# Softmax row sums of an attention kernel: from fifteen additions on GpSimd to block sums on VectorE, with more split tiles and one buffer less

## What is computed

```
kv = concatenate([context, latents], axis=1)              # 1857 keys
q = rms_norm((latents @ Wq) split into 32 heads, q_norm_w)
k = rms_norm((kv @ Wk) split into 8 heads, k_norm_w)
v = (kv @ Wv) split into 8 heads
scores = einsum('bhgqd,bhkd->bhgqk', q, k) / sqrt(128)
probs = softmax(scores)
out = einsum('bhgqk,bhkd->bhgqd', probs, v) ... @ Wo
```

## Time and profile before

| | us |
|---|---|
| median of three timed runs | 2815.78 (2813.55 to 2817.94) |
| the profiled execution, its own time | 2816.99 |
| its span, first to last instruction | 2815.2 |

### The profile page before, as it was taken

The page is one execution under the profiler, slowest core; times in us unless marked ns, Lnnn a source line. Parts: engine busy times, 40 slices in busy tenths (PEclk is TensorE's granted clock), DMA queues, the critical chain, the costliest instruction groups (busy, mean ns, idle before and its releaser), DMA issues.

```text
span 2815.2 us, 47816 instructions
## 1 busy us (share of the span) xinstructions
PE 2720.3 (97%) x14812; PEld 2220.4 (79%) x14812; DVE 2221.7 (79%) x3596; ACT 2029.4 (72%) x3945; POOL 2377.3 (84%) x2320
## 2 busy tenths in 40 slices
PE   7899999999999999999999999999999999999974
PEld 5777878777878888888888888888888888888853
DVE  5577888888778878888778887787778888788873
ACT  3577777777767777777777777777777777777771
POOL 4399999898888888878889988888898888888893
PEclk9999999999999999999999999999999999999996
DMA  6756565565555454555545455554455445344310
GB/s 234 253 184 216 193 221 193 195 213 184 183 178 200 160 177 169 182 177 196 178 147 193 167 189 174 179 184 165 156 173 173 154 158 180 124 165 150 117 42 26
DMA packets 159434, 485.64 MB, mean 173 GB/s; under 512 B 16839, under 2 KB 27849, under 8 KB 159182
## 3 DMA queue, kind: packets, MB, share of 16 engines
q1 hardware_dynamic: 157592, 481.01, 50.5%
q10 hardware_dynamic: 1590, 1.58, 0.2%
HBM read 403.09 MB, written 79.43 MB: 171 GB/s over the span
## 4 chain that ended last, share of the span: by engine, by line
PE 79%; POOL 9%; issue 6%; DVE 4%; ACT 2%; DMA 1%; SPq 0%; POOLq 0%; ACTq 0%; DVEq 0%
PE K_ps L971 9%; PE K_ps L973 9%; PE K_ps L972 9%; PE OT_ps L1001 7%; PE S_ps L971 6%; PE S_ps L973 6%; PE S_ps L972 6%; POOL acc L906 5%; PE OT_ps L971 5%; PE OT_ps L972 4%; PE OT_ps L973 4%; POOL P_lo L888 2%; PE F_ps L971 2%; PE F_ps L972 2%; PE F_ps L973 2%
## 5 line engine op out<-in xcount | busy, mean ns | idle before, releaser
L906 POOL TENSOR_TENSOR acc<-acc,scores 128x512 f32<-128x512 f32 (+1 forms) x832 | 1120.8, 1347 | 40.4 <-ACT scores L1323 10.1
L888 POOL TENSOR_TENSOR P_lo<-scores,P_hi 128x512 fp32r<-128x512 f32 x672 | 898.4, 1337 | 211.3 <-ACT scores L1323 210.3
L1652 DVE SCALAR_TENSOR_TENSOR running_max<-S_ps,rk,running_max 128x512 f32<-128x512 f32 (+1 forms) x896 | 669.0, 747 | 250.2 <-ACT scores L1309 247.8
L1636 DVE TENSOR_TENSOR scores<-scores,Mb_ps 128x512 f32<-128x512 f32 (+1 forms) x960 | 648.7, 676 | 134.4 <-PE Mb_ps L1127 134.3
L1309 ACT ACTIVATE scores<-S_ps,rk 128x512 f32<-128x512 f32 (+1 forms) x960 | 651.6, 679 | 139.8 <-PE S_ps L973 120.1
L1323 ACT ACTIVATE scores<-scores 128x512 f32<-128x512 f32 (+1 forms) x960 | 596.9, 622 | 59.2 <-DVE scores L1636 57.1
L1322 ACT ACTIVATE P_hi<-scores 128x512 fp32r<-128x512 f32 x672 | 423.1, 630 | 293.7 <-DVE scores L1636 213.9
L971 PE MATMUL S_ps<-QT_hi,KT_hi 128*128 128x512 f32 (+1 forms) x960 | 496.9, 518 | 14.8 <-DVE running_max L1652 13.0
L971 PE MATMUL K_ps<-Wkv_hi,kvT 128*128 128x256 f32 (+1 forms) x1664 | 470.9, 283 | 2.4 <-DVE kvT L1709 2.4
L973 PE MATMUL K_ps<-Wkv_hi,kvT 128*128 128x256 f32 (+1 forms) x1664 | 471.1, 283 | 0.0
L972 PE MATMUL K_ps<-Wkv_lo,kvT 128*128 128x256 f32 (+1 forms) x1664 | 470.3, 283 | 0.0
(11 more groups left out here) (226 smaller groups left out, 4666.8 us busy)
## 6 DMA issues: line engine op xcount, KB each, us to landing
kvT<-kvT_scratch SPq DMA_DIRECT2D x403, 512.0 KB, 3.7
Wq_hi<-weight_halves_scratch SPq DMA_DIRECT2D x48, 512.0 KB, 5.4
Wq_lo<-weight_halves_scratch SPq DMA_DIRECT2D x48, 512.0 KB, 6.6
Wo_hi<-weight_halves_scratch SPq DMA_DIRECT2D x48, 512.0 KB, 4.7
Wo_lo<-weight_halves_scratch SPq DMA_DIRECT2D x48, 512.0 KB, 5.6
kvT_scratch<-built SPq DMA_DIRECT2D x45, 512.0 KB, 4.3
rinv_spread<-rinv_scratch SPq DMA_DIRECT2D x64, 256.0 KB, 4.8
Wkv_hi<-weight_halves_scratch SPq DMA_DIRECT2D x24, 512.0 KB, 5.6
```

The lines of the kernel that those rows point to most:

```text
L888: e.tensor_tensor(P_lo[n % PB][0:r, :], prob(t)[0:r, :], f(P_hi[n % PB][0:r, :]), ALU.subtract)\
L906: e.tensor_tensor(a[0:r, :], a[0:r, :], prob(t)[0:r, :], ALU.add).then_inc(s_acc, 1)
L1636: e.tensor_tensor(d, d, Mb_ps[0:r, :], ALU.add).then_inc(s_d, 1)
L1652: e.scalar_tensor_tensor(a, src, k, a, ALU.mult, ALU.max).then_inc(s_top, 1)
```

## The change

- **Sums.** Of the 15 tiles of a half, three (`SUMMED`) are no longer added by POOL. DVE reduces each by a reduction that transposes blocks of 32 by 32 (`sum_tile`): for every 32 partitions, the 512 columns become 16 sums on 32 partitions. POOL adds the other twelve into `acc` (11 additions), and DVE reduces `acc` in the same way and then the four results to one 128x16 array (`sum_blocks`).
- **Jobs.** `AT` is now one small PE product of that array with a constant `same`; DVE takes the reciprocal straight out of PSUM into `rrow`. `RT` is gone, and store, spread, `divide`, `OT_high` and `OT_low`, which hung on `RT`, hang on `AT`, two steps sooner.
- **Split tiles.** `FULL` names 5, 3, 1 and 1 tiles, so 10, 12, 14 and 14 are split.
- **Events.** The later self-attention is placed by a table of its own, `LIGHT`, three places a half in the first two batches.
- **Buffer.** One `built` buffer instead of two; ACT waits for the last store before it writes the next tile.

```diff
-    FULL = [[2, 3, 6, 7, 10, 11, 14], [4, 5, 10, 11, 14], [6, 7, 14], [6, 7, 14]]
+    FULL = [[4, 5, 10, 11, 14], [6, 7, 14], [14], [14]]
+    SUMMED = [[2, 7, 13], [2, 9, 12], [3, 7, 11], [3, 7, 11]]
+    LIGHT = [[2, 7, 11], [2, 7, 12], [], []]
...
-            12: [("RT", 2 * v - 3)],
...
-            27: [("RT", 2 * v - 2), ("QT", v, 1)],
+            27: [("QT", v, 1)],
...
     def divided(s):
-        return [x[1] for x in fill(s - 6) if x[0] == "RT"]
+        return [x[1] for x in fill(s - 6) if x[0] == "AT"]
...
-        if j in FULL[p // 2] and j - 1 not in FULL[p // 2] and j < NJ - 1:
+        if j in LIGHT[p // 2]:
             EVENTS.append(s)
...
-                if j == 0:
+                if t not in ADD_AT:
                     return
...
-            def turn_sums(p):
-                e.wait_ge(s_acc, acc_no(NJ * p + NJ - 1))
+            def add_blocks(p):
+                if p == 0:
+                    e.wait_ge(s_same, 1)
+                e.wait_ge(s_bt, p + 1)
                 out = take(("AT", p))
-                for i in range(4):
-                    ins = e.transpose(out[:, i * P:(i + 1) * P], acc[p % 2][:, i * P:(i + 1) * P], ident[:])
-                ins.then_inc(s_ff, 1)
+                e.matmul(out[0:16, 0:32], sums[:, p % 2, :], same[:], start=True, stop=True).then_inc(s_ff, 1)
...
-                            e.wait_ge(s_xs[(k - 2) % 6], 16 * ((k - 2) // 6 + 1))
-                            dst = built[k % 2][:, 0, :, 0:r]
+                            if k > CTX:
+                                e.wait_ge(s_xs[(k - 1) % 6], 16 * ((k - 1) // 6 + 1))
+                            dst = built[:, 0, :, 0:r]
...
-                    e.reduce_sum(sums[:, p % 2, :], out.rearrange("p (i k) -> p i k", k=P), AX.X).then_inc(s_fr, 1)
-                    e.wait_ge(s_fr, F_AT[job] + 1)
-                    e.reciprocal(rinv[:, p % 2, :], sums[:, p % 2, :]).then_inc(s_ri, 1)
+                    if p:
+                        e.wait_ge(s_rd, 16 * p)
+                    e.reciprocal(rrow[:], out[0:16, 0:32]).then_inc(s_fr, 1)
...
+            def sum_tile(t):
+                p, j = divmod(t, NJ)
+                e.wait_ge(s_p, t + 1)
+                e.tensor_reduce(blocks[:, p % 2, SUMMED[p // 2].index(j), :], prob(t).rearrange("p (j a) -> p j a", a=32), AX.X,
+                                ALU.add, apply_transpose=True).then_inc(s_bs, 1)
+
+            def sum_blocks(p):
+                n = len(SUMMED[p // 2])
+                e.wait_ge(s_acc, ADD_AT[NJ * p + NJ - 1] + 1)
+                e.tensor_reduce(blocks[:, p % 2, n, :], acc[p % 2][:].rearrange("p (j a) -> p j a", a=32), AX.X,
+                                ALU.add, apply_transpose=True).then_inc(s_bs, 1)
+                e.wait_ge(s_bs, BLOCK_AT["acc", p] + 1)
...
+                e.reduce_sum(sums[:, p % 2, :], blocks[:, p % 2, 0:n + 1, :].rearrange("p k j -> p j k"), AX.X)\
+                    .then_inc(s_bt, 1)
...
+                if 0 <= s - WAIT - 1 < NS and summed_tile(s - WAIT - 1):
+                    sum_tile(s - WAIT - 1)
+                for x in fill(s + 1):
+                    if x[0] == "AT":
+                        sum_blocks(x[1])
                 for p in divided(s - 2):
                     OT_low(p)
```

More of the change, by code:

```diff
@@ L71, in layer @@
     TOP = 8
[L72 removed]
+    FULL = [[4, 5, 10, 11, 14], [6, 7, 14], [14], [14]]
+    SUMMED = [[2, 7, 13], [2, 9, 12], [3, 7, 11], [3, 7, 11]]
+    LIGHT = [[2, 7, 11], [2, 7, 12], [], []]
     FULL = [FULL[v // KVH] for v in range(UNITS)]
+    SUMMED = [SUMMED[v // KVH] for v in range(UNITS)]
+    LIGHT = [LIGHT[v // KVH] for v in range(UNITS)]
+    ADDED = [NJ * p + j for p in range(HALVES) for j in range(1, NJ) if j not in SUMMED[p // 2]]
+    ADD_AT = {t: n for n, t in enumerate(ADDED)}
     HALF = [[j for j in range(NJ) if j not in FULL[v]] for v in range(UNITS)]
@@ L312, in left @@
         return NJ * (2 * v - 3) + max(kind[v - 2][at]) + 1 if kind[v - 2][at] else 0
+    BLOCKS = []
+    for s in STEPS:
+        if 0 <= s - WAIT - 1 < NS and summed_tile(s - WAIT - 1):
+            BLOCKS.append(s - WAIT - 1)
+        BLOCKS += [("acc", x[1]) for x in fill(s + 1) if x[0] == "AT"]
+    BLOCK_AT = {x: n for n, x in enumerate(BLOCKS)}
     with ExitStack() as ctx:
@@ L400, in layer @@
         xrow = sb("xrow", [P, E])
-        built = [sb(f"built{i}", [P, 2, C, P], F32R) for i in range(2)]
+        built = sb("built", [P, 2, C, P], F32R)
         ident = sb("ident", [P, P])
@@ L404, in layer @@
         nm = sb("nm", [P, 2, 4])
-        sums = sb("sums", [P, 2, 4])
-        rinv = sb("rinv", [P, 2, 4])
-        rrow = sb("rrow", [4, P])
+        blocks = sb("block_sums", [P, 2, max(map(len, SUMMED)) + 1, 16])
+        sums = sb("block_totals", [P, 2, 16])
+        same = sb("same_in_block", [P, 32])
+        rrow = sb("rrow", [16, 32])
         rb_all = sb("rinv_spread", [P, QW])
@@ L703, in store_tile @@
                 k = x_no(b, n)
-                src = tile[k % 3] if b == 0 else built[k % 2]
+                src = tile[k % 3] if b == 0 else built
                 e.wait_ge(s_fr, F_AT["X", b, n] + 1)
@@ L1706, in drain @@
                         k = x_no(b, n)
-                        to = tile[k % 3] if b == 0 else built[k % 2]
+                        to = tile[k % 3] if b == 0 else built
                         hi, dst = to[:, 0, :, 0:r], to[:, 1, :, 0:r]
```

54 lines of the change are left out of this document (26 added, 28 removed).

## The result

The changed kernel takes 2842.5 us (median of 4 runs, 2837.6 to 2847.9), against 2816.7 us for the kernel before in runs beside it. The ratio is 1.0095 (95% interval 1.0077 to 1.0113): slower by about 1%, where 2792 us and faster had been forecast. The time lies above the forecast range and has the other sign.

A forecast was written before the change was run, and what follows sets the result against it. PE's work was taken as the bound up to about 2670 us, then POOL's pace in the tail. From 2817.0 us, 52 of gains off and 28 of stalls added gave 2793, as median 2792 us; forecast 2776 to 2809, 8-in-10 range 2762 to 2815.

The forecast's parts named there:

- 1.35 us for six cycles, 8 us: First batch, step 18: PE waits for the maximum, with only 0.35 us of slack before; 8 us lost.
- its 0.9: Third and fourth batch, step 18: PE waits 0.9 us a cycle for the maximum, bounds 0 and 1.5.
- 0.60 if POOL isn't in its way, 1.6 if it is, so 1.1: DVE, step 16: price in us of the division moved ahead of the shift and maximum.
- The sums: PE: four transposes of `acc` go, 0.44 us a half, 26.8 us over 61 halves.
- they cancel to within 0.1 us: PE: the dropped transpose of `RT` against the new small f32 product, priced at 0.12 us.
- The tiles: PE: two more split tiles a half, 0.16 us saved each, 19.5 us before the tail.
- The tail: Last three halves and end: one POOL instruction less a half, 3.7 us, and 2 us off the closing chain.
- The third and fourth batch: Step 18: PE stalls in 16 cycles, 14.4 us, plus 1.8 us where the router's copies share the step.
- Slow turning: Rival, 12%: a transposing reduction on DVE costs 1.28 us or more; 2837 us, range 2828 to 2850.
- Given back: Rival, 13%: PE's stalls reach their upper bound or beyond, 45 to 55 us, and take the gain; 2809 to 2820 us.
- Not PE: Rival, 3%: PE, relieved of work, only waits longer; the time stays near 2816 us.
- was not the bound there, so this counts nothing: POOL before the tail: some 85 us less work, counted as no gain.

The follow-up runs named there:

- run 6: The changed kernel with the old full and split tiles, so the new sums without the new tiles: 2822.0 us.
- run 7: The kernel before with the new full tiles, the new `LIGHT` places and one `built` buffer, old sums and division: 2873.5 us.
- run 1: The changed kernel with the division two steps later, in steps 18 and 3 of the cycle as before the change: 2840.2 us.
- run 4: The changed kernel with POOL's weight difference Wo_lo in step 17 of the cycle instead of 15: 2828.9 us.
- run 5: The changed kernel with POOL's weight differences of steps 11 and 15 cut to 64 of 1024 columns, the rest left out: 2819.3 us.
- run 8: The changed kernel with the block sum of tile 8 instead of 7 and weight difference Wo_lo in step 17 instead of 15: 2820.8 us.

## Why the prediction was wrong

**The step that failed** is "In the first batch the slack was smaller ... so I take 1.35 us for six cycles, 8 us". It named the right place and the wrong price. The measured loss to step 250 is 35.6 us, and 43 with the gains of 7.4 us (14 halves x 0.53) that are in it; some 4 of the 43 belong to the opening. The 1.35 us don't follow from the prediction's own terms either: with 0.35 us of slack instead of 1.06, its 0.9 becomes 1.6, and the division met POOL's weight difference in seven cycles by step 250, not six. Four things were left out:

- *The division's price was a mean.* "0.60 if POOL isn't in its way, 1.6 if it is, so 1.1" is a mean of two cases, near the 1.19 us that the division has over all batches. In the first batch POOL has instructions of 1024 columns and 2.4 us, and in all seven cycles the division, moved two steps ahead, met one: 2.54 to 2.56 us.
- *The query norms were taken as unchanged.* They have 3.37 us in the third batch. In the first batch they took 2.50 us on average before (units 1 to 6, 1.27 to 3.25) and take 4.51 in the changed kernel, 2.0 us more in each cycle, though the change didn't touch them. The two lines of unit 5 in the kernel before, DVE and POOL:

```profile
476.27 3.00 DVE L1675 TENSOR_TENSOR natq<-natq,rq 128x512 f32<-128x512 f32 x2
474.63 2.38 POOL L945 TENSOR_TENSOR Wq_lo<-w_stage,Wq_hi 128x1024 fp32r<-128x1024 f32 x1
```

There the norms began 1.64 us after POOL's difference, with 0.74 of it left. In the changed kernel they wait 0.40 us for `rq`, POOL's instruction just ahead of the difference, and so start 0.08 us after the difference and meet all of it. In run 6, which differs from the changed kernel only in the split tiles, they take 2.7 to 3.1 us in units 1 to 6; in run 7, with the tiles and without the block sums, 4.0 to 4.6. So this collision comes with the new split tiles. Runs 1 and 4, which shorten the division alone, leave 32.9 and 23.1 us of loss at step 250; run 5, which shortens both differences, leaves 7.2. So both collisions together are the cause of 28 of the 35.6 us, and by the difference from run 4 up to 16 of them go with the norms. No run shortened the norms alone.

- *The three things in one gapless stretch.* Block sum, division and a piece of the later self-attention add up in step 16. The piece was allowed for in the upper bound only; it takes 1.74 us in unit 5.
- *What comes after a wait.* The sum had only the wait itself. The waits of over 1 us for the maximum from step 40 to 250 are 27 us together. Windows of 200 us from 100 to 700 show clocks of 0.97, 0.97 and 0.96 where the kernel before has 0.99, 1.00 and 1.00; 0.02, 0.03 and 0.04 of 200 us each are 18 us, an estimate of what the lower clock costs. The middle one of the changed kernel is this row; that of before stands with run 7:

```profile
300.00:500.00 200.00, 190.01 (x1011) 154.80 (x1009) 172.99 (x259) 142.51 (x273) 170.16 (x158) 0.97 0.57 191
```

Between steps 40 and 250 the account nearly closes: 23.7 us more of waits and an estimate of 17 us for the lower clock (mean 0.973 over 622 us), less the 7.4 of gains, are 33 us, and the stretch is 32.0 us longer.

**The sums** were sized at 0.44 us a half and gave 0.22 (run 6), 13 us less in 61 halves. The step "they cancel to within 0.1 us" failed: sixteen products in a row don't tell what a single small one costs between two large ones.

**What held.** The tiles: 0.17 us each against 0.16. The block sum: 0.70 us. The Trainium skill (Vector Engine (DVE) Microarchitecture Reference, The reshape front-end and per-opcode configuration), cited for the lower price, agrees with the trace there. POOL has 82 us less (85 forecast) and DVE stands at 84%; ACT has 53 us more, less than the 81 of the `P_hi` alone. The tail: 3.9 us less from step 940 on against 5.7. The third and fourth batch: the stall is 1.3 us a cycle in the third (0.22 us longer a cycle, with 0.66 from tiles and 0.44 from sums in it), and about 0.4 in the fourth, where 0.9 were taken for each: two misses that nearly cancel in the sum. PE waits in the third batch exactly where it was said:

```profile
1764.58 0.70 DVE L1820 TRANSPOSE_TENSOR_REDUCE block_sums<-scores 128x16 f32<-128x512 f32 x1
1765.21 1.53 DVE L1838 TENSOR_TENSOR OT_n<-OT_n,rinv_spread 128x512 f32<-128x512 f32 x1
1766.66 0.68 DVE L1650 TENSOR_TENSOR scores<-scores,Mb_ps 128x512 f32<-128x512 f32 x1
...
1768.05 0.50 PE L985 MATMUL S_ps<-QT_hi,KT_hi 128*128 128x512 f32 x1 [1.10 <-DVE running_max L1666]
```

These are the DVE and PE timelines of unit 20, to be read against the earlier trace rows. The one `built` buffer makes PE wait 3.07 us in step 12, where 3 were allowed but not added:

```profile
115.77 0.60 ACT L1384 ACTIVATE built<-F_ps 128x512 fp32r<-128x512 f32 x1 [5.21 <-DMA kvT_scratch<-built]
...
117.80 0.79 PE L985 MATMUL S_ps<-QT_hi,KT_hi 128*128 128x512 f32 x1 [3.07 <-DVE running_max L1666]
```

How much of it is loss isn't fixed by these traces. The ten steps ahead of it took 20.3 us here and 22.8 in the kernel before, at mean clocks of 0.93 and 0.80. In runs 6 and 8, with the same buffer, they took 22.9 and the wait is 1.6 us, and run 6 has lost nothing by step 40.

**The rivals.** "Slow turning" has the measured time within its range (2828 to 2850), but by luck: its mechanism is false, with 0.70 us far under the 1.1 from which it decides. "Given back" had the mechanism, stalls beyond their upper bound, and stopped at 2820 us with the same price for the division. "Not PE" falls: where PE doesn't wait, what it is relieved of comes off the end. The sentence that POOL "was not the bound there, so this counts nothing" is wrong for the first batch: in run 7, without the block sums, waits for `P_lo` and for POOL's `rq` come up there, and in the changed kernel those for `P_lo` don't (1.7 us between steps 40 and 250).

**What stays open.** Why the second batch loses 15 us with the sums alone and gains 2 with sums and tiles; what the query norms cost by themselves; and what the one buffer costs in the opening.
